# Where a tile's combine-weight turns stand among the dispatch sums and logits on TensorE

## What is computed

```python
logits = (einsum('tzd,ed->tze', x, phi_w) + phi_b)     # x: layer-normed tokens; 64 experts x 32 slots
D = softmax(logits, axis=3)                            # dispatch weights, over a token's slots of one expert
C = softmax(logits, axis=2)                            # combine weights, over the experts
X_tilde = einsum('tznp,tzd->npd', D, x)                # dispatch sums, over all tokens
X_tilde = tanh(layernorm(clip(X_tilde)))
Y_tilde = einsum('npd,ndH->npH', X_tilde, expert_w) + expert_b
Y = einsum('tznp,npH->tzH', C, Y_tilde)                # combine
h = h + Y
```

## Time and profile before

| | us |
|---|---|
| median of three runs | 988.93 (988.03 to 990.25) |
| profiled execution | 990.47 |
| its span, first to last instruction | 988.8 |

### The profile page before, as it was taken

One profiled execution on the slowest core, in us unless ns is written; L12 is line 12 of the kernel. 1 busy time (PEld: TensorE's weight loads), 2 busy tenths in 40 slices (PEclk: granted clock), 3 DMA queues, 4 the chain that ended last, 5 costly groups with the idle time before them and its releaser, 6 DMA issues. The chain is left out here.

```text
span 988.8 us, 22780 instructions
## 1 busy us (share of the span) xinstructions
PE 923.2 (93%) x8222; PEld 788.1 (80%) x8222; DVE 712.5 (72%) x1047; ACT 502.7 (51%) x817; POOL 540.0 (55%) x494
## 2 busy tenths in 40 slices
PE   4889999999997858799999999999999989999997
PEld 3778888888885546688888888888888749999997
DVE  1356777777773598899999999999998754454452
ACT  1155555555554244566676667667665253333331
POOL 2265222222221177699999999999998452100100
PEclk9899999999997778899999999999999999999999
DMA  8311111111111042233323322332336995677660
GB/s 315 99 31 43 43 42 42 42 42 42 42 35 39 14 105 55 61 84 97 86 69 87 95 70 73 95 90 63 88 86 239 363 400 202 220 231 240 213 186 17
DMA packets 97907, 110.89 MB, mean 112 GB/s; under 512 B 12180, under 2 KB 89012, under 8 KB 91716
## 3 DMA queue, kind: packets, MB, share of 16 engines
q1 hardware_dynamic: 95908, 105.46, 34.5%
q0 software_dynamic: 1376, 3.70, 1.0%
q10 hardware_dynamic: 576, 1.11, 0.3%
HBM read 72.04 MB, written 38.21 MB: 111 GB/s over the span
## 5 line engine op out<-in xcount | busy, mean ns | idle before, releaser
L1224 PE MATMUL slots_p_sum<-slots_x,slots_disp 128*128 128x256 f32 (+1 forms) x928 | 206.9, 380 | 2.2 <-DVE xacc L933 2.2
L1224 PEld LDWEIGHTS slots_p_sum<-slots_x,slots_disp 128*128 128x128 f32 (+1 forms) x928 | 173.4, 190 | 26.9 <-issue 4.2
L1029 POOL TENSOR_TENSOR slots_comb<-slots_comb,slots_cmax 128x1024 f32<-128x1024 f32 (+1 forms) x58 | 111.7, 1944 | 11.4 <-DVE slots_cmax L908 10.3
L1040 POOL TENSOR_TENSOR slots_comb<-slots_comb,slots_csum 128x2048 f32<-128x2048 f32 (+1 forms) x29 | 104.9, 3619 | 19.1 <-DVE slots_csum L862 19.1
L1251 PE MATMUL slots_logits<-phi_hi,slots_xt_hi 128*128 128x512 f32 (+1 forms) x232 | 84.2, 446 | 19.7 <-DVE slots_xt_lo L888 19.7
L1034 POOL TENSOR_TENSOR slots_disp<-slots_disp,slots_dsum 128x2048 f32<-128x2048 f32 (+1 forms) x28 | 102.1, 3646 | 0.0
L398 POOL TENSOR_TENSOR attend_stack<-attend_rope_a,attend_rope_b 113x128 f32<-113x128 f32 x128 | 54.4, 457 | 80.4 <-DVE attend_rope_b L353 80.4
L1068 POOL DMA_DIRECT2D out<-slots_o x29 | 15.9, 548 | 149.0 <-DVE slots_o L970 149.0
L876 DVE TENSOR_TENSOR slots_disp<-slots_logits,slots_dmax 128x512 f32<-128x512 f32 (+1 forms) x116 | 80.2, 691 | 4.2
L1081 ACT ACTIVATE slots_ct<-slots_p_turn 128x512 f32<-128x512 f32 (+1 forms) x116 | 63.9, 577 | 31.1 <-PE slots_p_turn L1212 31.1
L871 DVE TENSOR_REDUCE slots_dmax<-slots_logits 128x16 f32<-128x512 f32 (+1 forms) x116 | 77.7, 669 | 0.0
(11 more groups left out here) (133 smaller groups left out, 1962.3 us busy)
## 6 DMA issues: line engine op xcount, KB each, us to landing
combine_t<-slots_ct SPq DMA_DIRECT2D x224, 128.0 KB, 2.4
slots_comb<-combine_t SPq DMA_DIRECT2D x14, 1024.0 KB, 5.5
slots_ct<-combine_t SPq DMA_DIRECT2D x14, 1024.0 KB, 6.1
expert_w<-wexp SPq DMA_DIRECT2D x8, 1024.0 KB, 9.9
slots_disp<-wexp SPq DMA_DIRECT2D x8, 1024.0 KB, 14.2
h<-attend_h_out SPq DMA_DIRECT2D x32, 113.0 KB
slots_h_t<-h SPq DMA_DIRECT2D x28, 128.0 KB, 2.3
slots_x<-h SPq DMA_DIRECT2D x28, 128.0 KB, 2.1
```

What stands on the lines that cost most here:

```text
L1029: nc.gpsimd.tensor_tensor(m, m, cmax[0:rows, shalf(i)].unsqueeze(2).broadcast_to([rows, SLOTS // 2, EXPERTS]), ALU.subtract).then_inc(csub ...
L1040: nc.gpsimd.tensor_tensor(m, m, csum[0:rows, 1].unsqueeze(2).broadcast_to([rows, SLOTS, EXPERTS]), ALU.mult).then_inc(comb_ok, 1)
L1224: last = nc.tensor.matmul(p_sum[u % 2][:, i, :], disp[d][0:rows].rearrange("p n s -> p (n s)")[:, 128 * e:128 * e + 128], x[d][0:rows], st ...
```

## The change

In the steps after the fourth, the turns of the combine weights are moved on TensorE: quarters 0 and 1 between the two blocks of the second unit of sums, quarters 2 and 3 behind the last sum, and the four banks of logits follow as one run. No instruction is added or taken away, and no other engine's program is changed.

```diff
-        def add_products(u, tiles, newest):
-            for i in range(2):
+        def add_products(u, tiles, newest, blocks=range(2)):
+            for i in blocks:
...
-        def multiply_group(t, c):
-            for s, u in sums(t, c):
+        def multiply_group(t, c, between):
+            for n, (s, u) in enumerate(sums(t, c)):
...
-                add_products(u, tiles, done).then_inc(sum_ok, 1)
+                if n == 0:
+                    add_products(u, tiles, done).then_inc(sum_ok, 1)
+                else:
+                    add_products(u, tiles, done, [0])
+                    between()
+                    add_products(u, tiles, done, [1]).then_inc(sum_ok, 1)
...
-            multiply_group(t, c)
-            woven = nxt and not early
+            def first_turns():
+                if not early:
+                    turn_weights(t - 1, c + 1, 0)
+                    turn_weights(t - 1, c + 1, 1)
+
+            multiply_group(t, c, first_turns)
             if not static(t) or t >= 1:
-                turn_weights(t - 1, c + 1, 0)
-                turn_weights(t - 1, c + 1, 1)
-                for q in (2, 3):
-                    if woven:
-                        multiply_logits(t, nrows, [q - 2])
-                    turn_weights(t - 1, c + 1, q)
-            if woven:
-                multiply_logits(t, nrows, [2, 3])
+                if early:
+                    turn_weights(t - 1, c + 1, 0)
+                    turn_weights(t - 1, c + 1, 1)
+                turn_weights(t - 1, c + 1, 2)
+                turn_weights(t - 1, c + 1, 3)
+            if nxt and not early:
+                multiply_logits(t, nrows, range(NB))
```

## The result

The changed kernel took 996.12 us (median of six runs, 995.43 to 996.75), the kernel before 989.33 us (six runs, 988.03 to 991.76) beside it: a ratio of 1.0065, 95% interval 1.0055 to 1.0075. It is slower by 6.8 us; 5.8 were forecast. As an absolute time 994.7 us had been forecast, counted from a median of 988.93 of the first three runs before. The profiled execution took 996.36 us with a span of 994.6, against 990.47 and 988.8.

A forecast was written before the change was run, and what follows sets the result against it. TensorE was taken to bound the steps at 14.46 us. 1.75 us for the start, 20 x 0.193 for the steady steps and 0.2 behind step 27 gave +5.8 us, median 988.93 to 994.7 us; range 990.5 to 998.3.

The forecast's parts named there:

- The spare time of 1.40 us: TensorE, steady steps: the first two quarters' operand from GpSimd is ready 1.40 us before they are turned.
- The ring: Unit 0's sums, ScalarE, VectorE, GpSimd, quarters' turn, next unit 0: 29.31 us over two steps, 0.19 us more a step.
- The start: Steps 5 and 6: TensorE waits for GpSimd's product with a block still to do; 1.50, then 1.75 us late in all.
- The last quarters: Quarters 2 and 3 on TensorE: the block of sums covers ScalarE's copies of quarters 0 and 1, by 0.2 us.
- The logits in one run and the changes between turns and logits: TensorE's work and VectorE's later bank 0: nothing taken for either in the steady steps.
- VectorE's wait ahead of the maxima: VectorE ahead of the combine maxima: near 0.6 us where it was 0.35, a sign of being right.
- the early records of 0.71 us: Logits behind turns on TensorE: first record starts 0.08 us early and gives nothing, so no saving.
- the rival "faster": TensorE: no binding wait, and turn-logit changes cost; 23 steps lose 0.16 us each, 985.2 us; chance 0.05.
- The rival "the same": Steady steps stay at 14.46 to 14.52 us, only steps 5 and 6 pay, 990.7 to 991 us; chance 0.13.
- The term for what lies behind step 27: VectorE's chain up to the last tile's maxima, with no slack: 0.2 us once for the later bank 0.
- The price of about 2 us for one fall: TensorE's clock falling once in step 5: some 2 us, 996.7 us; with the second-wait case, chance 0.12.
- the rival of the swinging clock: Steady steps: short holes make TensorE's clock swing, every second step losing 2 us, 1016 us; chance 0.02.

The follow-up runs named there:

- half a block: Changed kernel, but quarters 0 and 1 in the middle of the last block of sums, 0.86 us ahead of their old place: 993.35 us, 1.0032 of before.
- Cutting the ring: Changed kernel, with ScalarE copying all four banks of logits first and unit 0's sums then: 993.46 us, ratio 1.0036 to the kernel before.
- The logits in one run alone: Kernel before, with quarters 2 and 3 straight behind 0 and 1 and the four banks of logits behind them: 1002.97 us, ratio 1.0134.
- The first-quarters kernel: Changed kernel, but only quarters 0 and 1 moved; quarters 2 and 3 and the banks woven as before: 996.56 us, ratio 1.0069 to before.
- the second comparison: Both kernels unchanged, profiled and timed again: changed 996.66 us, ratio 1.0071; kernel before 989.48 us, ratio 1.0004.
- the two-block kernel: Changed kernel, but quarters 0 and 1 between the two units of sums, two blocks ahead of their old place: 1030.95 us, 1.0408 of before.
- the copies first in before: Kernel before, with ScalarE copying all four banks of logits ahead of unit 0's sums: 989.45 us, ratio 0.999.
- the three kernels with two blocks: Quarters 0 and 1 two blocks early: as such 1030.95 us; with bank 0 ahead of quarter 2, 1019.70; with ScalarE copying the banks first, 1031.31.

## Why the prediction was right

It was right in its mechanism and in most terms.

- **The spare time of 1.40 us**, the number it turned on, held: a block (1.73 us) is too much for the steady steps and half a block (0.87 us) is not.
- **The ring.** Its first link was given as 16.32 us and measured 16.32, the way back through TensorE as 12.94 and measured 12.94. Twenty steps took 293.31 us against 293.10. The pairs of 14.48 and 14.85 us, named as a possibility, are there. Cutting the ring gave 14.46 us again.
- **The start.** +1.50 us in step 5 was right to the hundredth, +0.25 in step 6 was +0.27. Together with the ring it is 324.71 us from step 5 to step 27 against 318.88, so +5.83, where 5.6 was forecast. The hole in step 5 shows as 1.73 us where the prediction has 1.98 in one place and 1.9 in another: the turn's weight load stands idle from further back (2.1 us in its own row).
- **The last quarters.** Called covered by 0.2 us; they waited once, for 0.2 us, in the whole of the steady steps. The logits in one run alone (1.34% slower), and step 5 with half a block, show what the wait costs where the cover is missing or short.
- **The logits in one run and the changes between turns and logits**: 0 for both. The first-quarters kernel, which has the old weaving, has the same steps, and the changed kernel with the ring cut has TensorE's old step. So the early records of 0.71 us were nothing to gain, and the rival "faster" falls. The rival "the same" falls with the ring's wait in every step.
- **VectorE's wait ahead of the maxima**: 0.6 us forecast; 0.39 and 0.56 us in the two steps shown, 11.0 us in 22 steps, 0.50 on the mean.

Two things were off. The term for what lies behind step 27 was 0.2 us; it measured 0.13 us up to the start of the last tile's maxima and another 0.7 to 1.3 us behind it, of which the slower sixteen passes are about 0.6. I took the 1.67 us of the earlier trace rows as the nearest row for the hole in step 5, which was right (the granted clock stayed at 1.00 from 421 to 430 us, behind 1.73 us idle), but did not look at TensorE's other long idle times behind the slot steps. Whether the change brings the fall there or only goes along with it is open. The price of about 2 us for one fall was near: the sixteen passes with 5.38 in place of 3.69 us lose 1.69. The sum, 5.83 + 0.13 + 0.7 to 1.3, is 6.7 to 7.3 us, and the medians differ by 6.8 and, on the second comparison, 7.4, so no larger term is missing.

The second is a step that was missing and did no harm. The one-step ring through bank 0 stood nowhere in the prediction. By estimate it is a block shorter in the changed kernel than in the two-block kernel, 16.03 - 1.73 = 14.30 us, 0.36 us under the 14.66 of the ring that I had found. That it stayed under was luck: with a little more in it the forecast would have been short, as it was for the two-block kernel.

## What to carry to other kernels

Before an instruction is moved ahead on the engine that sets the pace, take from the trace how long its operand has been ready, and compare that with the work it is moved past; then follow the operand back, and if it comes from this engine's own earlier work, add up the whole loop and divide by the number of steps it spans: over the engine's own step it costs in every round, under it only once. Look for every loop that the moved place closes, not for the first only. Where the order must be so, such a loop can be cut on an engine with time to spare (here by ScalarE's order of copies), though what that shifts elsewhere has to be read too: with the loop cut, the changed kernel still was 0.36% slower than the kernel before.

## What the runs showed that I had not expected

- An idle of the same 2.08 us, at the same place in the program, was followed by full speed in four profiles of three kernels (before twice, the logits in one run, the copies first in before: 1.07 us for sixteen passes, granted clock 1.00 over the 2 us from their start) and by a lowered clock in ten profiles of the nine others (1.19 to 1.93 us, granted clock 0.50 to 0.71). In the 6 us ahead of the passes it was 0.98 to 1.00 in all fourteen. Within a kernel profiled twice it came out the same both times. What decides it is open. Idles of 1.35 to 1.81 us ahead of the sums at 760 to 780 us never lowered it (3.69 us for sixteen passes), 2.28 and 2.31 us did (5.38), and so did 3.49 to 3.50 us in step 5 of the three kernels with two blocks (5.30 to 5.31 us in place of 3.62). So in two kernels an idle 0.6 us longer than before was followed by 1.7 us lost.
- The short holes of the changed kernel, up to 0.4 us in every second step ahead of turns into p_turn0 and p_turn1, left the granted clock at 1.00 from 430 to 740 us. So the rival of the swinging clock, which had stood on the Trainium skill (TensorE: Matmul & The Clock Gate, "A second HAM failure mode: psum-queue depth-cycling"), did not come up in this kernel.
- The profile's busy row of TensorE shows 0.29 us idle in 50 where the steps are 0.7 us longer in the same stretch: part of such a wait is in the weight load's row and not in the matmul's.
